# Expert layers: shift rows put in place by transfers on ScalarE's queue, scores follow their maxima by 24 units in place of 32

## The reference

```python
hn = _layernorm(x, ln1_g, ln1_b)               # x is (4, 512, 128), 16 heads of 8
q, k, v = heads(hn @ wq + bq), heads(hn @ wk + bk), heads(hn @ wv + bv)
scores = jnp.einsum('bhqd,bhkd->bhqk', q, k) / jnp.sqrt(jnp.float32(D))
attn = jax.nn.softmax(scores, axis=-1)
o = jnp.einsum('bhqk,bhkd->bhqd', attn, v)
x = x + (o @ wo + bo)
hn2 = _layernorm(x, ln2_g, ln2_b).reshape(-1, h)
idx = jnp.argmax(hn2 @ gate_w + gate_b, axis=-1)      # one of 8 experts for each token
mid = jax.nn.relu(jnp.einsum('th,ehf->etf', hn2, w1) + b1[:, None, :])
y = jnp.einsum('etf,efh->eth', mid, w2) + b2[:, None, :]
return x + y[idx, tokens]
```

## Time and profile before

| | us |
|---|---|
| median of 3 runs | 1418.21 |
| lowest, highest | 1416.77, 1423.64 |
| the profiled execution's own time | 1411.51 |
| its span, first to last instruction | 1409.6 |
| first expert layer, first maximum to last score | 312.2 to 550.6 |
| second expert layer, the same | 1092.9 to 1331.6 |

### The profile page before, as it was taken

The page is one execution under the profiler, slowest core; times in us unless marked ns, Lnnn a source line. Parts: engine busy times, 40 slices in busy tenths (PEclk is TensorE's granted clock), DMA queues, the critical chain, the costliest instruction groups (busy, mean ns, idle before and its releaser), DMA issues. The chain is left out here.

```text
span 1409.6 us, 32943 instructions
## 1 busy us (share of the span) xinstructions
PE 1137.5 (81%) x12906; PEld 615.4 (44%) x12906; DVE 987.8 (70%) x2114; ACT 687.5 (49%) x1412; POOL 631.2 (45%) x838
## 2 busy tenths in 40 slices
PE   6747758769999998853778888979875899999975
PEld 2212323323333334842456666666664333333375
DVE  5699999968888884536856664746621888888453
ACT  3843334424776667531362352452430277676754
POOL 2369979955234312531363353453451623342153
PEclk9968889977999999876798988999998699999988
DMA  5377934121241402235133232232111233150222
GB/s 158 125 287 308 353 122 173 56 73 49 63 91 50 122 6 87 65 99 100 24 66 74 41 60 68 36 78 60 33 20 33 64 77 87 39 132 10 85 58 88
DMA packets 132799, 127.63 MB, mean 91 GB/s; under 512 B 86295, under 2 KB 117847, under 8 KB 128122
## 3 DMA queue, kind: packets, MB, share of 16 engines
q1 hardware_dynamic: 124592, 117.65, 29.6%
q0 software_dynamic: 2496, 5.13, 1.1%
q10 hardware_dynamic: 5558, 2.76, 1.0%
HBM read 104.83 MB, written 37.90 MB: 101 GB/s over the span
## 5 line engine op out<-in xcount | busy, mean ns | idle before, releaser
L1400 DVE TENSOR_REDUCE f_row_min<-f_ps 128x1 f32<-128x512 f32 x512 | 327.3, 681 | 62.5 <-PE f_ps L1720 62.0
L1282 ACT ACTIVATE f_e<-f_ps 128x512 f32<-128x512 f32 x512 | 278.5, 598 | 122.8 <-PE f_ps L1739 117.1
L1720 PE MATMUL f_ps<-f_operands 72*128 72x512 bf16 x512 | 205.2, 412 | 20.1 <-DMA f_operands<-k_scr 15.2
L1739 PE MATMUL f_ps<-f_operands 75*128 75x512 bf16 x512 | 189.5, 380 | 2.6 <-ACT f_e L1282 2.1
L790 PE MATMUL m_ps<-m_shared,sb_ident 128*128 128x512 f32 x256 | 139.4, 695 | 55.0 <-DVE m_shared L630 54.8
L363 POOL TENSOR_TENSOR m_drive<-m_du,m_ring 128x1024 f32<-128x1024 f32 x64 | 149.6, 2350 | 54.6 <-DVE m_ps L622 36.8
L495 ACT ACTIVATE m_ps<-m_delta,m_A 128x511 f32<-128x511 f32 x128 | 83.0, 681 | 130.8 <-DVE m_ps L622 109.0
L1750 PE MATMUL f_ps<-f_e,f_v_op 128*32 128x512 f32 x1024 | 136.4, 604 | 2.4 <-ACT f_e L1282 1.4
L2545 DVE TENSOR_REDUCE d_row_min<-d_ps 128x1 f32<-128x384 f32 (+3 forms) x176 | 104.5, 632 | 28.2 <-PE d_ps L2768 27.1
L1720 PEld LDWEIGHTS f_ps<-f_operands 72*128 72x128 bf16 x512 | 51.3, 101 | 162.0 <-DVE f_row_min L1400 110.4
L790 PEld LDWEIGHTS m_ps<-m_shared,sb_ident 128*128 128x128 f32 x256 | 53.5, 219 | 143.3 <-DVE m_shared L630 84.5
(11 more groups left out here) (297 smaller groups left out, 2169.7 us busy)
## 6 DMA issues: line engine op xcount, KB each, us to landing
m_ring<-bc_scr SPq DMA_DIRECT2D x32, 1024.0 KB, 5.2
f_rows_scr<-blank SPq DMA_DIRECT2D x2, 8707.5 KB, 31.2
f_wall<-f_wall SPq DMA_DIRECT2D x16, 578.0 KB
f_operands<-q_scr SPq DMA_DIRECT2D x32, 288.0 KB
f_operands<-k_scr SPq DMA_DIRECT2D x96, 96.0 KB
d_q_op<-q_scr SPq DMA_DIRECT2D x12, 288.0 KB
d_k_op<-k_scr SPq DMA_DIRECT2D x36, 96.0 KB
f_operands<-f_rows_scr SPq DMA_DIRECT2D x46, 64.5 KB, 1.8
```

What stands on the lines that cost most here:

```text
L1282: nc.scalar.activation(e_sb[:, n % 3, hh, :], ps[:, SCORE[(b * UNITS + u) % SCORE_BANKS], :], ACT.Exp, scale=SCALE).then_inc(s["e_out"], 1)
L1400: nc.vector.tensor_reduce(row_min[:, b % 2, u // TPB, u % TPB:u % TPB + 1], ps[:, MAXQ[(b * UNITS + u) % MAX_BANKS], :], AX.X, ALU.max, ne ...
L1720: nc.tensor.matmul(ps[:, MAXQ[n % MAX_BANKS], :], q_op(b, QK)[:, hd, t * P:(t + 1) * P], k_op(b, QK)[:, hd, :], start=True, stop=True).the ...
L1739: nc.tensor.matmul(ps[:, SCORE[n % SCORE_BANKS], :], k_op(b, QKS)[:, hd, t * P:(t + 1) * P], q_op(b, QKS)[:, hd, :], start=True, stop=True ...
```

## The change

LAG goes from 32 to 24. The score of unit u then stands in slot u + 24: slots 24 to 31 gain a score each, slots 280 to 287 hold none, and everything placed by the score's unit (exponentials, `weighted`, `leave`) moves eight slots up while everything placed by slot stays. The DMA of the shift rows leaves SyncE's loop and becomes `shifts` of ScalarE, two slots behind the turning of the maxima, one behind their copy. SyncE waits for the third quarter's landing ahead of the second half of the operand loads, and for the fourth's ahead of the weights.

```diff
-LAG = 32
+LAG = 24
@@ SyncE
-                def shifts(b, k):
-                    sp.wait_ge(s["m_out"], QUARTERS * b + k + 1)
-                    sp.dma_start(q_op(b, slice(QK_ROWS, SHIFT_ROWS))[:, quarter_heads(k), :].rearrange("j h (t s) -> j (h t) s", t=TPB),
-                                 max_part[:, k, :]).then_inc(m_in[k], 16)
-
@@
                 for b in range(B):
-                    shifts(b, 0)
-                    shifts(b, 1)
                     if b + 1 < B:
                         store_parts(b + 1)
                         for g in range(GROUPS // 2):
                             load_group(b + 1, g)
-                    shifts(b, 2)
-                    if b + 1 < B:
+                        sp.wait_ge(m_in[2], 16 * (b + 1))
                         for g in range(GROUPS // 2, GROUPS):
                             load_group(b + 1, g)
-                    shifts(b, 3)
                     if b >= 1:
+                        sp.wait_ge(m_in[3], 16 * (b + 1))
                         load_walls((b - 1) * E // 4)
@@ ScalarE
+                def shifts(b, k):
+                    act.wait_ge(s["m_out"], QUARTERS * b + k + 1)
+                    if b >= 2:
+                        act.wait_ge(s["s_ps"], (b - 2) * UNITS + (k + 1) * IN_QUARTER)
+                    act.dma_start(q_op(b, slice(QK_ROWS, SHIFT_ROWS))[:, quarter_heads(k), :].rearrange("j h (t s) -> j (h t) s", t=TPB),
+                                  max_part[:, k, :]).then_inc(m_in[k], 16)
@@
                     if due(i - 1, AT_TURN_MAXIMA):
                         shifts_leave(*due(i - 1, AT_TURN_MAXIMA))
+                    if due(i - 2, AT_TURN_MAXIMA):
+                        shifts(*due(i - 2, AT_TURN_MAXIMA))
```

## The result

The changed kernel takes 1441.86 us (median of 6 runs, 1432.40 to 1444.95) against 1420.62 (6 runs, 1416.77 to 1433.46): a ratio of 1.0114, 95% interval 1.0073 to 1.0155. By that ratio it is slower by 1.1%, 16 us; the two medians themselves stand 21.2 us, 1.5%, apart. Forecast were +3.1 us and no measurable change, with a range of 1411 to 1431; the result lies above it. The profiled execution took 1432.40, with a span of 1430.6, 21.0 more than before's.

A forecast was written before the change was run, and what follows sets the result against it. TensorE was taken to set the pace where maxima and scores run together. The terms 5.0 - 6.3 + 2.0 + 0 + 0 + 2.4 gave +3.1 us, 1421.3 on the median of 1418.21, range 1411 to 1431.

The forecast's parts named there:

- One place is worse: First batch's third-quarter shift rows share DMA engines with operand loads: a stall of 1.2 us a layer, +2.4 us.
- Part 1, front: Slots 24 to 31 gain scores while TensorE is already gapless at half clock: +5.0 us, 2.5 a layer.
- Part 2, back: Eight score slots fall away behind slot 279, but `turn_out` is limited by tile 1's landing: -6.3 us.
- Part 3, ScalarE's order: `leave` ahead of `attended` at slot 43 delays `project_out`, +3.0 us; sooner maxima copies return 1: +2.0 us.
- Part 4, issue: 32 transfer issues move to ScalarE, whose slack absorbs them while exponentials run on: 0 us.
- The rival of 1437 to 1449: ScalarE's issues stop the exponentials at slots 20, 36, 53 and 68 of each batch: +19 to +31 us, chance 0.14.
- The forecast's own sign: Forecast wrong if the combined stretch of maxima and scores, 192 us before, changes by more than 3 us.
- The other two: Further signs: scores at quarter starts wait all along; ScalarE gaps of 0.7 us behind each issue return as idle TensorE.

The follow-up runs named there:

- e3: The changed kernel with the first batch's loads of the next operands held until the third quarter's shift rows have landed; 1449.98 us, ratio 1.0142 to before.
- e2: The kernel before with only the lag cut to 24, shift rows left on SyncE's queue; 1446.31 us, ratio 1.0146 to before.
- e10: e9 plus extra matmuls with unread results in slots 4 to 23, one, two or eight a slot; 1448.92 us, one run.
- e6: e5 plus ScalarE making `attended` ahead of `leave` at slot 43; 1435.42 us, one run.
- e1: The changed kernel with the lag put back to 32, transfers still on ScalarE's queue; 1424.15 us, ratio 0.9992 to before.
- e9: e6 with the first batch's last group of operand loads held until the fourth quarter has landed; 1434.11 us, ratio 1.0075 to before.
- e4: The changed kernel with a lag of 28; 1429.21 us, ratio 1.0026 to before.
- e7: The changed kernel with one extra matmul, its result unread, in each of slots 6 to 23; 1437.72 us, one run.
- e5: The changed kernel with, in the first batch, one group of operand loads ahead of the third quarter's landing and three behind; 1446.7 us, one run.
- e8: The changed kernel with the edits of e6 and e7 together; 1441.59 us, ratio 1.0139 to before.

## Why the prediction was wrong, step by step

Terms for both expert layers together, against the marks of the two profiled executions:

| term | forecast (ends) | measured |
|---|---|---|
| front, to slot 32 | +5.0 (+1.3 to +7.0) | +6.8 |
| slots 32 to 56 | 0 | +0.8 |
| first batch's third quarter, slots 56 to 64 | +2.4 (0 to +6.4) | +10.7 |
| slots 64 to 255, `attended` behind `leave` among them | +2.0 (0 to +3) | +4.1 |
| slot 255 to `turn_out` | -6.3 (-9.6 to -4.3) | -7.2 |
| behind `turn_out` | 0 | +3.7 |
| sum | +3.1 | +18.9 |

- **The step that failed is the last of Part 4**, "One place is worse". The mechanism was named and its place was right, slot 56 of the first batch. The size was not: 1.2 us a layer, at most 3.2, against 5.4 and 5.3. Two parts of it were too small.
  - The landing was taken at 1.7 or 1.8 us and "1 to 3 us more". It took 5.4 and 5.0, and TensorE stood idle for 3.65 and 3.50 us, over the upper end. That end let the transfer "wait out that busy stretch to 359". Here the loads ahead of it begin 2.7 us later than before, and slot 56 comes 3.0 later, so 359 stands for about 362, and the last packet did land at 362.2. The end was nearly the right value, and the 1.2 was not. The packets in the trace of the kernel before held it: 5.46 and 4.92 us for this transfer.
  - The price of an idle TensorE was put at its length alone. Behind it the clock was half for 3.4 us in each layer (363.51 to 366.92, 1155.40 to 1158.82), about 1.7 us more, half of that stretch.

  e3 shows that the loads are the cause, and e2 that a queue of its own does not remove them. With 10.7 us in place of 2.4 the sum would have been +11.4, 1429.6 on before's median, still inside the range. The other terms below took the result out of it.
- **Part 1, front**: 6.8 against 5.0, near the upper end of 7.0, whose reasoning (half clock until about 336, as before) is what happened. The choice "above the middle" was too low. e10's second layer shows the full-clock figure to be right too. Slots 32 to 56, put at 0, took another 0.4 us in each layer, at slot 40, where the first batch's second quarter waits 0.24 and 0.19 us for its rows.
- **Part 2, back**: right in the mechanism and the sum. The tiles are the limit (0.77 us of idle time for `f_rows_scr` in the first layer, 1.47 in the second), and 7.2 of a possible 9.6 us came back. The split was not as forecast: 3.9 and 3.3 us, for 2.3 and 4.0.
- **Part 3, ScalarE's order**: the 0.49 us at `project_out`, three times a layer, are 2.9 as foreseen, and e6 takes them away. Of the 1 us that the copies should give back 0.6 came: 0.16 at slots 103 and 167 of each layer, where `weighted` had stood 0.09 us waiting for the group's copy. The rest of the 4.1 us is two places that the sum didn't have. The third quarter of the third batch waits a little too (0.5 and 0.3 us by slot 185). And once, in the second layer, the turning of the maxima waits for ScalarE's copy of the values, which ScalarE began after 2.52 us without work; why it began so late is open:
```profile
1267.35 0.22 PE L1727 MATMUL f_ps<-sb_ident_b,f_min_part 128*48 128x128 bf16 x1 [1.13 <-ACT f_v_op L1265]
```
- **Part 4, issue**: right at 0. e1 has all 32 issues on ScalarE and no loss, and the exponential goes on under an issue. The rival of 1437 to 1449 thus had the right time by luck: its mechanism did not happen.
- **Not in the sum**: 3.25 us behind `turn_out` in the second layer, 0.45 in the first. The clock is half behind `turn_out` in the kernel before as well, but later and for less: in its second layer the first stretch begins 10.3 us behind `turn_out`, and two stretches of 3.4 and 6.8 us stand ahead of the one in which the layer ends. In the changed kernel the first begins with `turn_out` (1353.38), and there are three (1353.38 to 1356.79, 1363.62 to 1370.44, 1377.27 to 1384.10). Whether the change brings this about is open. The same stretch of e1, whose lag is 32, lost 0.0 and 1.9 us, that of the other runs with a lag of 24 lost 0.4 to 4.6.
- **The rest of the sum**: without the failed term and what lies behind `turn_out` the measured terms give +4.5 us, where the same terms were forecast at +0.7, low too but by less. With the loads moved out of the way (e9) the layers come to +4.0, near the +3.1 forecast; but e9's median is 7.9 us over before's. Its profiled execution, span 1419.3, was the fastest of its six. That trace has another 5.7 us over before's outside the expert layers, in unchanged code; what the slower executions lost has no trace and is left open.
- **The forecast's own sign** of being wrong came: the stretch from slot 32 to 255 changed by 7.5 and 8.1 us, where 3 were allowed. The other two, scores that wait all along and gaps of 0.7 us behind each issue, did not.

## What to carry to other kernels

Where the same engine sets the pace in the middle and at both ends, a shorter pipeline lag only moves work from the tail to the front: here 3.4 us of a gain of 3.3 to 3.9 a layer went into the front. What it surely does is cut every deadline inside, so list the tightest producer-to-consumer distances and ask which transfers are in flight at each. A small transfer that must land in a few microseconds wants no bulk load issued ahead of it on any queue; space the loads between such transfers (e9), and count an idle stretch of TensorE at its length plus the half clock that may follow. Read how long a transfer takes now, even where nobody waits for it: a shorter lag uncovers it.

## What the runs showed of the hardware

- 12 KB issued with two groups of operand loads (1.15 MB) just ahead of them took 4.9 to 5.8 us to the last packet in the kernels with a lag of 24 or 28 and in the kernel before; on the loads' own queue 4.9 to 5.5 (before, e2), on another 5.0 to 5.8 (the changed kernel, e4, e7). In e1 it was 3.5 and 4.7. In the changed kernel's other 30 transfers it is 1.6 to 2.1.
- A gapless TensorE does not by itself bring the full clock: in e10's first layer it stayed half to 352.86, and TensorE was busy 35.00 of 35 us from 318 to 353. In e5, e7 and the changed kernel it fell to half behind idle times of 1.28, 1.54 and 3.65 us. The length of the idle time alone doesn't decide: it stayed full behind 1.32 us in e6, 1.34 in e8 and 1.40 in e10's second layer, and in e4's second layer it fell (1311.50) behind 0.84, which left it full in the kernel before.
- The same code differs much between executions. The layer between the two expert layers, of before, of the changed kernel and of e1, windows:
```profile
624.00:1093.00 469.00, 360.90 (x9037) 264.47 (x9038) 256.50 (x723) 165.63 (x369) 182.46 (x513) 0.87 0.29 56
```
```profile
631.00:1103.00 472.00, 362.86 (x9006) 269.78 (x9038) 256.37 (x723) 165.46 (x369) 181.90 (x513) 0.85 0.29 56
```
```profile
624.00:1109.00 485.00, 380.67 (x9037) 280.10 (x9038) 256.27 (x724) 165.51 (x369) 181.70 (x512) 0.82 0.28 54
```
The other engines' busy times agree to 1 us; the granted clock is what differs, and the layer takes 469 to 485 us, with 117, 141 and 174 us at half clock. Over all twelve traces it is 467 to 490 us. A single execution thus says little of a change of 1%. Marks inside the changed stretch do, and medians of several runs.
